# A two-block transformer kernel on one core: one plain fp32 matmul per dense product in place of three matmuls over high and low halves

## The chip, the core and the metric

The kernel runs on one NeuronCore of a Trainium2 chip. Five engines work side by side, each with a program of its own, and meet only at semaphores: TensorE (PE, matmuls and transposes, with weight loads shown apart as PEld), VectorE (DVE), ScalarE (ACT), GpSimd (POOL) and SyncE (SP, which starts the DMAs). The metric is device time in microseconds of one launch. Time before: 4109.65 us, the median of three runs between 4104.24 and 4113.88.

## What is computed

There are 16 sequences of 512 tokens and 256 channels. Each goes through two residual blocks, cut here to what matters:

```python
x = x + attn(layernorm(x))      # 16 heads of 16 channels: q, k, v = x @ Wq.T, x @ Wk.T, x @ Wv.T
                                # layernorm of q and k per head, causal softmax, out @ Wo.T + bo
x = x + ffn(layernorm(x))
# ffn: y = y + latent attention(rmsnorm(y)): q = y @ Wq (16 heads of 64),
#      ckv = y @ Wkva (64 wide), causal softmax, Wkvb, @ Wo
#      y = y + shared expert + sum over the 2 chosen of 8 experts, each silu(y @ Wg) * (y @ Wu) @ Wd
```

All inputs and outputs are fp32. The dense products are the q, k, v and output projections of both attentions, the gate's logits, and the nine experts (one shared, eight routed). The kernel computes all nine for all tokens and weighs them.

## The kernel before

One sequence is one pass of a loop ("batch" b, 16 passes; the last one is written out apart). Tokens lie in NT = 4 tiles of 128, channels in KC = 2 halves of 128. The weights are loaded, scaled and centred once before the loop, and stay in SBUF. Every engine runs its own hand-written order, and semaphores (the `Signal` objects) tie them.

**How a dense product is made.** PE has two ways to take fp32 data. Tiles declared `F32R` go in as one instruction. Tiles declared `F32` go in as a plain fp32 matmul. Here every dense operand is held twice, as a high half (a copy rounded to fp32r) and a low half (what is left over), and a product is the sum of three fp32r matmuls, `TERMS`: high by high, high by low, low by high. The weights' halves are made before the loop (ACT copies at L811, DVE subtractions at L1016). The tokens' halves are made three times per batch, after PE has transposed the normalised tokens into PSUM: ACT copies `xth` (L818), DVE subtracts `xtl` (L1032). The halves of an attention's output are `oth` (ACT, L851) and `otl` (POOL, L462; the last of four by DVE, L1087), from `onm` (L1068). Those of an expert's hidden layer are `hidh` (ACT, L958) and `hidl` (DVE, L1218), from `hid` (L1214).

**A batch on PE, in order.** (1) `project_qk` (L566) and `project_v` (L575) for four token tiles; `transpose_stack` (L590). (2) `attend` for the first attention: scores (L602, L608), transposes of the probabilities (L619), `weigh_values` (L630), sums (L639), then `project_out` (L671). (3) `transpose_tokens` (L551), then eight `project_q` (L691), each with a `transpose_q` (L704) of two steps earlier, and one `project_kv` (L679). (4) `attend` for the second attention with scores at L606 and L607, then `project_out`. (5) `transpose_tokens`, the gate (L777), and the experts: `gate_up(e + 1)` (L717, two products of 256 by 512 tokens) stands ahead of `down(e)` (L729). Next to `down(8)` stands the transposition of the next batch's tokens.

**What the other engines do beside it.** ACT: exponentials (L833), every third to fourth copy of a probability block (L841), SiLU (L954). DVE: row maxima (L1049), the other block copies (L1057), and per expert `hid`, `hidl` and four additions into `x1` (L1230). POOL: the powers of -1/2 (L449), the spread of the sums (L457), rotary sums (L499) and the key's parts (L506 to L516).

`weigh_values` (L630) and the two products that fold weights before the loop (L537, L542) already use plain fp32 tiles (`va`, `vb`, `probt`; `r_wqt`, `r_kvbt`, `r_wob`). In the trace a plain fp32 matmul stands as two MATMUL records with a weight load each, and an fp32r matmul as one: L630 issues 2560 matmuls in each attention over the run, and the trace has 5120 records for each.

## Time and profile before

| what | value |
|---|---|
| median of three runs | 4109.65 us |
| span of the profiled execution | 4099.4 us |
| PE busy | 3512.7 us (86%), 31392 matmul records |
| DVE busy | 3056.1 us (75%) |
| ACT busy | 2303.1 us (56%) |
| POOL busy | 776.0 us (19%) |
| length of one batch (the second, by the returning pattern of instructions) | 249.2 us |
| start of the first matmul of batch 0 | 86.56 us |

The page has one line per engine with its busy time, a chain of work that ended last with each engine's share of it, and groups of instructions by source line. A matmul's duration includes its way through the array, so consecutive matmuls overlap in the records, and the distance between two starts tells what one costs. PEclk is the clock that PE was granted, as a share of 2.4 GHz: 1.00 is 2.4 GHz and 0.50 is 1.2 GHz.

### The profile page before, as it was taken

The page shows a single profiled execution, that of the slowest core. Times are in us where ns is not written, and L with a number is a line of the kernel's source. Part 1 is how long each engine was busy: PE and PEld are TensorE (multiplying, and loading weights), DVE is VectorE, ACT ScalarE, POOL GpSimd, SP SyncE. Part 2 cuts the span into 40 slices and gives each one's busy share as a digit, 9 for nine tenths or more (in the row PEclk, how much of TensorE's full clock was granted, in tenths as well). Part 3 has the DMA queues.
Part 4 walks back from the last instruction along what each step waited for, and adds up shares of the span by engine and source line. Part 5 has one row for each costly group of instructions (what it writes and reads, how often), then busy time and mean ns, then how long its engine had stood idle before and what let it go on. Part 6 is the DMA issues. An engine that isn't in the chain of part 4 may idle for free.

```text
span 4099.4 us, 93010 instructions
## 1 busy us (share of the span) xinstructions
PE 3512.7 (86%) x31392; PEld 2772.0 (68%) x31392; DVE 3056.1 (75%) x6444; ACT 2303.1 (56%) x6346; POOL 776.0 (19%) x919
## 2 busy tenths in 40 slices
PE   3898988989889898898988889888898988989888
PEld 2676766767667676676766767666676766767667
DVE  3878777787777877768787787877778777787776
ACT  2656546565465664646655465654656546565464
POOL 1212222022120221212122121222202212022120
PEclk9999999999899999999999999998999989999899
DMA  3000000000000000000000000000000000000000
GB/s 73 7 2 7 7 7 7 2 7 7 7 7 1 8 6 7 7 7 7 2 7 7 7 7 2 7 7 7 7 2 7 7 7 7 2 7 7 6 1 6
DMA packets 33906, 30.35 MB, mean 7 GB/s; under 512 B 8864, under 2 KB 33312, under 8 KB 33376
## 3 DMA queue, kind: packets, MB, share of 16 engines
q1 hardware_dynamic: 33376, 23.68, 2.0%
q8 instruction: 284, 4.65, 0.5%
q14 instruction: 246, 2.02, 0.2%
HBM read 15.28 MB, written 8.39 MB: 6 GB/s over the span
## 4 chain that ended last, share of the span: by engine, by line
PE 56%; issue 14%; DVE 13%; ACT 10%; POOL 5%; SPq 1%; ACTq 0%; DMA 0%; DVEq 0%; POOLq 0%
PE bank L619 12%; PE scores L717 9%; ACT prob L833 6%; PE bank L630 6%; PE scores L606 6%; PE bank L729 5%; PE scores L607 4%; PE scores L608 3%; POOL qf L499 2%; PE scores L691 2%; PE scores L671 2%; PE scores L602 2%; PE bank L590 2%; DVE negmax L1049 1%; DVE stk L1145 1%
## 5 line engine op out<-in xcount | busy, mean ns | idle before, releaser
L833 ACT ACTIVATE prob<-scores,negmax 128x128 f32<-128x128 f32 (+3 forms) x2048 | 1060.8, 538 | 223.6 <-DVE negmax L1049 180.2
L1049 DVE TENSOR_REDUCE negmax<-scores 128x1 f32<-128x128 f32 (+3 forms) x2048 | 884.5, 483 | 102.0 <-PE scores L608 88.4
L619 PE MATMUL bank<-ident,prob 128*128 128x128 f32 x5120 | 731.2, 280 | 44.5 <-DVE probt L1057 35.1
L1057 DVE COPY probt<-bank 128x512 f32<-128x512 f32 x896 | 596.6, 683 | 180.1 <-PE bank L619 173.1
L619 PEld LDWEIGHTS bank<-ident,prob 128*128 128x128 f32 x5120 | 548.6, 142 | 155.5 <-DVE probt L1057 65.9
L606 PE MATMUL scores<-khh,qt 128*128 128x256 f32 (+2 forms) x1024 | 439.2, 430 | 13.3 <-issue 6.6
L608 PE MATMUL scores<-mask,ident 128*128 128x128 bf16 x2048 | 450.4, 231 | 0.0
L833 ACT ACTIVATION_READ_ACCUMULATOR prob<-scores,negmax 128x1 f32 x2048 | 438.0, 214 | 0.0
L804 ACT ACTIVATE probt<-bank 128x512 f32<-128x512 f32 x384 | 233.0, 607 | 205.3 <-PE bank L619 205.3
L607 PE MATMUL scores<-kll,qt 128*128 128x256 f32 (+2 forms) x1024 | 346.1, 338 | 0.0
L590 PE MATMUL bank<-ident,stk 128*96 128x128 bf16 x2048 | 206.9, 288 | 149.8 <-DVE stk L1147 119.7
L717 PE MATMUL scores<-xth,wgu 128*128 128x512 f32 x1152 | 328.2, 407 | 0.0
L602 PE MATMUL scores<-qkt 96*128 96x128 bf16 (+3 forms) x1024 | 266.5, 306 | 45.9 <-DVE qkt L1037 13.9
L590 PEld LDWEIGHTS bank<-ident,stk 128*96 128x96 bf16 x2048 | 191.4, 178 | 166.0 <-DVE stk L1147 78.1
L608 PEld LDWEIGHTS scores<-mask,ident 128*128 128x128 bf16 x2048 | 205.4, 100 | 141.4 <-issue 110.7
L462 POOL TENSOR_TENSOR otl<-onm,oth 128x512 fp32r<-128x512 f32 x96 | 122.6, 1277 | 897.0 <-ACT oth L804 897.0
L717 PEld LDWEIGHTS scores<-xth,wgu 128*128 128x128 f32 x1152 | 214.0, 194 | 43.8
L954 ACT ACTIVATE sg<-scores 128x512 f32<-128x512 f32 x144 | 86.3, 599 | 279.0 <-PE scores L717 279.0
L457 POOL COPY rexp<-rsum 128x512 f32<-128x512 f32 x128 | 78.3, 612 | 859.7 <-DVE rsum L1061 859.7
L449 POOL TENSOR_TENSOR rstd<-var,expo 128x4 f32<-128x4 f32 x64 | 66.9, 1052 | 898.3 <-DVE var L1109 551.6
L729 PE MATMUL bank<-wd,hidh 128*128 128x256 f32 x1152 | 212.0, 282 | 27.4 <-ACT hidh L804 21.8
L606 PEld LDWEIGHTS scores<-khh,qt 128*128 128x128 f32 x1024 | 221.1, 216 | 17.9 <-issue 9.6
(178 smaller groups left out, 6937.0 us busy)
## 6 DMA issues: line engine op xcount, KB each, us to landing
x_in<-in_x_rows SPq DMA_DIRECT2D x16, 512.0 KB, 3.5
out_rows<-x SPq DMA_DIRECT2D x16, 512.0 KB, 3.5
r_gu<-in_wg SPq DMA_DIRECT2D x2, 512.0 KB, 5.1
r_gu<-in_wu SPq DMA_DIRECT2D x2, 512.0 KB, 5.1
r_d<-in_wd SPq DMA_DIRECT2D x1, 1024.0 KB, 6.5
r_wqt<-in_wq_nope_t SPq DMA_DIRECT2D x1, 512.0 KB, 6.8
r_wqr<-in_wq SPq DMA_DIRECT2D x2, 256.0 KB, 8.6
r_wob<-in_wo SPq DMA_DIRECT2D x1, 512.0 KB, 5.3
```

The lines of the kernel that those rows point to most:

```text
L590: ins = nc.tensor.transpose(out[0:SD, i * P:(i + 1) * P], stk[:, t % 2, quad * 8 + i].rearrange("p s d -> p (s d)"), ident16[:, :])
L602: mm(bank[q][:, 0:n], qkt[:, h, j * P:(j + 1) * P], qkt[:, H + h, 0:n], start=True, stop=False)
L606: mm(bank[q][:, 0:m], tok, khh[:, 0:m], start=True, stop=False)
L607: mm(bank[q][:, 0:m], tok, kll[:, 0:m], start=False, stop=False)
L608: ins = mm(bank[q][:, n - P:n], ident16[:, :], mask16[:, :], start=False, stop=True)
L619: ins = nc.tensor.transpose(bank[4 + n % 2][:, q * P:(q + 1) * P], prob[:, u % 2, q, i * P:(i + 1) * P], ident[:, :])
L630: ins = mm(bank[6][q * HP:(q + 1) * HP, j * P:(j + 1) * P], val, probt[:, u % 2, i, q * P:(q + 1) * P], start=i == 0, stop=i == j)
L717: ins = mm(bank[2 * s + w][:, :], wgu[:, w_, e, k, w * I:(w + 1) * I], XT[x_][:, k], start=m == 0 and k == 0, stop=m == 2 and k == KC - 1)
L729: ins = mm(bank[4 + 2 * s + t // 2][:, (t % 2) * C:(t % 2 + 1) * C], (hidh, hidl)[x_][:, s, t * P:(t + 1) * P], wd[:, w_, e], start=m == 0 ...
L833: nc.scalar.activation(prob[:, u % 2, q, 0:n], bank[q][:, 0:n], ACT.Exp, bias=negmax[:, a, u, q:q + 1], accum_out=sums[:, a, u, q:q + 1]). ...
L1049: nc.vector.tensor_reduce(negmax[:, a, u, M * part:M * part + M], scores[:, M * part:M * part + M, 0:n], axis=AX.X, op=ALU.max, negate=Tru ...
L1057: nc.vector.tensor_copy(probt[:, u % 2, i], bank[4 + n % 2][:, :]).then_inc(probt_dve.sem, 1)
```

## The change

Every dense weight becomes one `F32` tile, and so do the transposed tokens (`xt`), an attention's output (`ot`) and the hidden layer (`hid`). A product is one plain fp32 matmul in place of three fp32r ones. The steps that made halves are gone: the ACT copies and DVE subtractions of the weights, `oth` and `otl`, `hidh` and `hidl`. DVE now writes `ot` where it wrote `onm`. The transposed tokens are copied once, half 0 by ACT and half 1 by DVE, and PE waits for each half where it first needs it. The weights are loaded straight into their final tiles, so the separate raw tiles are gone as well. The attentions' own matmuls (scores, transposes, `weigh_values`) are as before. `weights_ready` is reached after DVE's last scaling (L1011). The core of the diff:

```diff
-    wqkv = new("wqkv", [P, 2, KC, 3 * C], F32R)
...
-    wgu = new("wgu", [P, 2, NE, KC, 2 * I], F32R)
...
+    wqkv = new("wqkv", [P, KC, 3 * C], F32)
...
+    wgu = new("wgu", [P, NE, KC, 2 * I], F32)
...
-    TERMS = ((0, 0), (0, 1), (1, 0))
...
-        sp.wait_ge(weights_ready, len(SPLIT))
+        sp.wait_ge(weights_ready, WEIGHTS)
...
-                if g == NG - 1:
-                    break
-                pool.wait_ge(oth_ready.sem, oth_ready.at(b, a * NG + g + 1))
-                nc.gpsimd.tensor_tensor(otl[:, g], onm[:, :], oth[:, g].bitcast(F32), ALU.subtract).then_inc(otl_ready.sem, 1)
...
-            for m, (x_, w_) in enumerate(TERMS):
-                if t == 0 and m == 2:
-                    lo_split(b, 0)
-                for k in range(KC):
-                    ins = mm(bank[t][:, :], XT[x_][:, k, t * P:(t + 1) * P], wqkv[:, w_, k, 0:2 * C],
-                             start=m == 0 and k == 0, stop=m == 2 and k == KC - 1)
+            for k in range(KC):
+                if t == 0:
+                    tokens_copied(b, 0, k)
+                ins = mm(bank[t][:, :], xt[:, k, t * P:(t + 1) * P], wqkv[:, k, 0:2 * C], start=k == 0, stop=k == KC - 1)
...
             for t in range(NT):
                 for g in groups:
                     if t == 0:
-                        pe.wait_ge(oth_ready.sem, oth_ready.at(b, a * NG + g + 1))
-                        pe.wait_ge(otl_ready.sem, otl_ready.at(b, a * NG + g + 1))
-                    for m, (x_, w_) in enumerate(TERMS):
-                        ins = mm(bank[t][:, 0:C], (oth, otl)[x_][:, g, t * P:(t + 1) * P], w[:, w_, g],
-                                 start=m == 0 and g == 0, stop=m == 2 and g == NG - 1)
+                        pe.wait_ge(ot_ready.sem, ot_ready.at(b, a * NG + g + 1))
+                    ins = mm(bank[t][:, 0:C], ot[:, g, t * P:(t + 1) * P], w[:, g], start=g == 0, stop=g == NG - 1)
                 if g == NG - 1:
                     ins.then_inc(y_psum.sem, 1)
...
             if e >= 2:
                 pe.wait_ge(hid_ready.sem, hid_ready.at(b, e - 1))
             for w in range(2):
-                for m, (x_, w_) in enumerate(TERMS):
-                    for k in range(KC):
-                        ins = mm(bank[2 * s + w][:, :], wgu[:, w_, e, k, w * I:(w + 1) * I], XT[x_][:, k],
-                                 start=m == 0 and k == 0, stop=m == 2 and k == KC - 1)
+                for k in range(KC):
+                    ins = mm(bank[2 * s + w][:, :], wgu[:, e, k, w * I:(w + 1) * I], xt[:, k], start=k == 0, stop=k == KC - 1)
             ins.then_inc(gate_up_psum.sem, 1)
 
         def down(b, e):
             s = e % 2
-            pe.wait_ge(hidh_ready.sem, hidh_ready.at(b, e + 1))
-            pe.wait_ge(hidl_ready.sem, hidl_ready.at(b, e + 1))
+            pe.wait_ge(hid_ready.sem, hid_ready.at(b, e + 1))
             if e >= 2:
                 pe.wait_ge(down_added.sem, down_added.at(b, e - 1))
             for t in range(NT):
-                for m, (x_, w_) in enumerate(TERMS):
-                    ins = mm(bank[4 + 2 * s + t // 2][:, (t % 2) * C:(t % 2 + 1) * C], (hidh, hidl)[x_][:, s, t * P:(t + 1) * P],
-                             wd[:, w_, e], start=m == 0, stop=m == 2)
+                ins = mm(bank[4 + 2 * s + t // 2][:, (t % 2) * C:(t % 2 + 1) * C], hid[:, s, t * P:(t + 1) * P], wd[:, e],
+                         start=True, stop=True)
                 if t % 2:
                     ins.then_inc(down_psum.sem, 1)
...
-        def split_tokens(b, stage):
-            for k in range(KC):
-                act.wait_ge(xt_psum.sem, xt_psum.at(b, stage * KC + k + 1))
-                copy(xth[:, k], bank[TOKEN_BANK[stage] + k][:, :]).then_inc(xth_ready.sem, 1)
+        def copy_tokens(b, stage):
+            act.wait_ge(xt_psum.sem, xt_psum.at(b, stage * KC + 1))
+            copy(xt[:, 0], bank[TOKEN_BANK[stage]][:, :]).then_inc(xt_act.sem, 1)
...
-        def split_out(b, a, g):
-            act.wait_ge(onm_ready.sem, onm_ready.at(b, a * NG + g + 1))
-            copy(oth[:, g], onm[:, :]).then_inc(oth_ready.sem, 1)
...
                 act.wait_ge(gate_up_psum.sem, gate_up_psum.at(b, e + 1))
+                if e >= 2:
+                    act.wait_ge(hid_ready.sem, hid_ready.at(b, e - 1))
                 nc.scalar.activation(sg[:, s], bank[2 * s][:, :], ACT.Silu).then_inc(silu_ready.sem, 1)
-                act.wait_ge(hid_ready.sem, hid_ready.at(b, e + 1))
-                if e >= 2:
-                    act.wait_ge(down_psum.sem, down_psum.at(b, 2 * (e - 1)))
-                copy(hidh[:, s], hid[:, s]).then_inc(hidh_ready.sem, 1)
...
-        for n, (raw, w, _) in enumerate(SPLIT):
-            dve.wait_ge(hi_ready, n + 1)
-            raw_ = raw[tuple([slice(None)] * len(raw.shape))]
-            tt(flat(w[:, 1]), flat(raw_), flat(w[:, 0]).bitcast(F32), ALU.subtract).then_inc(weights_ready, 1)
+            ins = ts(wgate[:, k], wgate[:, k], r_ln[:, 1, k:k + 1], None, ALU.mult)
+        ins.then_inc(weights_ready, 1)
...
-        def split_tokens(b, stage):
-            for k in range(KC):
-                dve.wait_ge(xth_ready.sem, xth_ready.at(b, stage * KC + k + 1))
-                tt(xtl[:, k], bank[TOKEN_BANK[stage] + k][:, :], xth[:, k].bitcast(F32), ALU.subtract).then_inc(xtl_ready.sem, 1)
+        def copy_tokens(b, stage):
+            dve.wait_ge(xt_psum.sem, xt_psum.at(b, (stage + 1) * KC))
+            nc.vector.tensor_copy(xt[:, 1], bank[TOKEN_BANK[stage] + 1][:, :]).then_inc(xt_dve.sem, 1)
...
-            if g > 0:
-                dve.wait_ge(otl_ready.sem, otl_ready.at(b, a * NG + g))
-            tt(onm[:, :], bank[7][:, :], osb[:, :], ALU.mult).then_inc(onm_ready.sem, 1)
+            tt(ot[:, g], bank[7][:, :], osb[:, :], ALU.mult).then_inc(ot_ready.sem, 1)
...
-            dve.wait_ge(oth_ready.sem, oth_ready.at(b, (a + 1) * NG))
-            tt(otl[:, NG - 1], onm[:, :], oth[:, NG - 1].bitcast(F32), ALU.subtract).then_inc(otl_ready.sem, 1)
...
-                    dve.wait_ge(hidh_ready.sem, hidh_ready.at(b, e + 1))
-                    if e >= 2:
-                        dve.wait_ge(down_psum.sem, down_psum.at(b, 2 * (e - 1)))
-                    tt(hidl[:, s], hid[:, s], hidh[:, s].bitcast(F32), ALU.subtract).then_inc(hidl_ready.sem, 1)
```

PE, in the experts: one `down` and the `gate_up` behind it, before (`scores` and `bank` are PSUM).

```order
L729 MATMUL bank<-wd,hidh 128x256 x2
L729 MATMUL bank<-wd,hidl 128x256
L729 MATMUL bank<-wd,hidh 128x256 x2
L729 MATMUL bank<-wd,hidl 128x256
L729 MATMUL bank<-wd,hidh 128x256 x2
L729 MATMUL bank<-wd,hidl 128x256
L729 MATMUL bank<-wd,hidh 128x256 x2
L729 MATMUL bank<-wd,hidl 128x256
L717 MATMUL scores<-xth,wgu 128x512 x4
L717 MATMUL scores<-xtl,wgu 128x512 x2
L717 MATMUL scores<-xth,wgu 128x512 x4
L717 MATMUL scores<-xtl,wgu 128x512 x2
```

The same place of the changed kernel, with the `gate_up` ahead of it and the next `down`:

```order
L632 MATMUL scores<-xt,wgu 128x512 x4
L637 REGISTER_ALU
L641 MATMUL bank<-wd,hid 128x256 x4
L632 MATMUL scores<-xt,wgu 128x512 x4
L637 REGISTER_ALU
L641 MATMUL bank<-wd,hid 128x256 x4
```

Twelve matmuls of 256 columns became four plain ones, and twelve of 512 columns became four; their order is the same.

ACT, at the end of the experts and the hand-over to the next batch, before:

```order
L954 ACTIVATE sg<-scores 128x512
L957 REGISTER_ALU
L804 ACTIVATE hidh<-hid 128x512
L817 ISA
L804 ACTIVATE xth<-scores 128x512
L817 REGISTER_ALU
L804 ACTIVATE xth<-scores 128x512
L961 ACT_TABLE_LOAD
```

And of the changed kernel:

```order
L847 ACTIVATE sg<-scores 128x512
L844 REGISTER_ALU
L847 ACTIVATE sg<-scores 128x512
L715 ISA
L710 ACTIVATE xt<-scores 128x512
L850 ACT_TABLE_LOAD
```

The copy between two SiLUs is gone, and one of the two token copies has moved to DVE.

## Rows read from the trace of the kernel before

**Rows 1.** Page, part 1: engine, busy us, share of the span, instructions.

```profile
PE 3512.7 (86%) x31392; PEld 2772.0 (68%) x31392; DVE 3056.1 (75%) x6444; ACT 2303.1 (56%) x6346; POOL 776.0 (19%) x919
```

**Rows 2.** Page, part 4: the chain that ended last, by engine.

```profile
PE 56%; issue 14%; DVE 13%; ACT 10%; POOL 5%; SPq 1%; ACTq 0%; DMA 0%; DVEq 0%; POOLq 0%
```

**Rows 3.** Table by stage, batch 1: stretch, length, busy us (instructions) of PE, PEld, DVE, ACT, POOL; granted clock.

```profile
333.90:366.20 32.30, 20.79 (x147) 18.30 (x148) 27.24 (x45) 17.50 (x34) 13.88 (x22) 0.75 0.06 19
366.20:423.50 57.30, 51.93 (x656) 37.16 (x654) 48.57 (x103) 45.18 (x148) 6.26 (x7) 0.99 0.01 2
435.60:459.30 23.70, 21.51 (x114) 17.02 (x114) 16.48 (x39) 12.18 (x26) 13.59 (x13) 0.94 0.00 0
468.60:526.80 58.20, 57.86 (x663) 44.14 (x661) 46.02 (x92) 41.30 (x133) 6.29 (x7) 0.99 0.01 2
548.07:577.70 29.63, 29.63 (x169) 25.80 (x170) 21.93 (x51) 8.10 (x14) 1.01 (x1) 1.00 0.00 1
```

**Rows 4.** Experts of batch 1: chain in order of time, then timeline with the wait in brackets.

```profile
556.74 1.41 PE bank L729 x12
558.15 2.80 PE scores L717 x12
...
548.07 0.48 PE L729 MATMUL bank<-wd,hidh 128*128 128x256 f32 x2 [0.56 <-DVE hidl L1218]
```

**Rows 5.** Timeline; single lines (forms, ns min/median/max, first and last start); table by stage.

```profile
276.69 1.08 PE L630 MATMUL bank<-probt,vb 128*32 128x128 f32 x32
...
L630 PE MATMUL bank<-probt,vb x320: 272/273/297, 221.9 to 277.5; 128*32 128x128 f32 x160
...
L729 PE MATMUL bank<-wd,hidh x72: 278/279/360, 548.1 to 582.7; 128*128 128x256 f32 x72
...
L542 PE MATMUL scores<-r_wob,r_kvbt x32: 629/629/630, 51.2 to 54.2; 32*32 32x256 f32 x32
...
L777 PE MATMUL scores<-xtl,wgate x2: 628/628/628, 539.5 to 539.9; 128*8 128x512 f32 x2
...
538.00:540.00 2.00, 2.00 (x6) 0.52 (x4) 1.74 (x3) 0.00 (x0) 0.00 (x0) 0.50 0.00 0
```

**Rows 6.** Timeline of PE before the first batch.

```profile
37.45 13.86 PE L537 MATMUL scores<-r_kvbt,r_wqt 32*128 32x32 f32 x64 [37.45 <-DMA r_woa<-in_wo1t]
```

**Rows 7.** Chain in order of time, before the first batch.

```profile
62.26 1.13 DVE woa L1016
...
76.00 0.10 DVE wgate L1016
```

**Rows 8.** Timeline of DVE beside the second output projection of batch 1.

```profile
529.08 0.69 DVE L1087 TENSOR_TENSOR otl<-onm,oth 128x512 fp32r<-128x512 f32 x1 [0.70 <-ACT oth L804]
```

**Rows 9.** Timeline where tokens go from PE through ACT and DVE back to PE.

```profile
434.48 1.09 ACT L804 ACTIVATE xth<-bank 128x512 fp32r<-128x512 f32 x2 [8.78 <-PE bank L551]
...
435.62 2.07 PE L691 MATMUL scores<-wq,xth 128*128 128x512 f32 x4 [0.96 <-ACT xth L804]
```

**Rows 10.** Timeline of the query projections, batch 1: the starts of two in a row.

```profile
449.65 1.18 PE L691 MATMUL scores<-wq,xth 128*128 128x512 f32 x4
...
451.91 1.18 PE L691 MATMUL scores<-wq,xth 128*128 128x512 f32 x4
```

**Rows 11.** Turn from batch 1 to batch 2: timeline, then chain.

```profile
581.45 0.47 PE L729 MATMUL bank<-wd,hidh 128*128 128x256 f32 x2 [1.36 <-ACT hidh L804]
...
583.10 2.38 issue
585.49 2.94 PE scores L566 x6
```

**Rows 12.** Timeline of ACT in the first attention of batch 1.

```profile
375.78 0.60 ACT L804 ACTIVATE probt<-bank 128x512 f32<-128x512 f32 x1
...
388.80 0.61 ACT L804 ACTIVATE probt<-bank 128x512 f32<-128x512 f32 x1
...
402.06 0.61 ACT L804 ACTIVATE probt<-bank 128x512 f32<-128x512 f32 x1
```

167 lines of the change are left out of this document (58 added, 109 removed).

## The prediction

> **What bounds the kernel now.** I began with the busy times and the chain that ended last. PE is busy for 86% of the span [rows 1], and 56% of the chain is PE's own work; DVE has 13%, ACT 10%, POOL 5% [rows 2]. So PE's work counts, but not everywhere, and the table by stage says where [rows 3]. In the experts PE is busy for all 29.63 us. In the second attention it is busy for 57.86 of 58.20 us, in the first for 51.93 of 57.30 us. In the stretch of the q, k, v projections and their norms (333.9 to 366.2) it is busy for 20.79 of 32.30 us only: there a chain through ACT, DVE and POOL sets the pace. In the query projections it is busy for 21.51 of 23.70 us. Last I read the chain inside the experts [rows 4]: `down` 1.41 us, `gate_up` 2.80 us, in turn and with nothing between.
>
> **What a plain fp32 matmul costs.** This decides the case. An fp32r `gate_up` is 12 matmuls of 512 columns in 2.80 us, 0.233 us each; a `down` is 12 of 256 columns in 1.41 us, 0.1175 us each [rows 4]. Both are 0.457 ns per column: call that one pass. `weigh_values` shows the plain form. Its row has 32 records for 16 matmuls, each of 128 columns over a strip 32 wide [rows 5]. Four strips run side by side, so the 32 starts make 28 steps: (1.08 - 0.27) / 28 = 0.029 us per record, or four times that, 0.116 us, for 128 columns in one strip. That is 0.90 ns per column and record, two passes, so two records are four passes. The durations agree: a plain record of 128 columns takes 273 ns and an fp32r one of 256 columns 279 ns [rows 5]. At the lower clock (granted 0.50, which is 1.2 GHz) an fp32r matmul of 512 columns takes 628 ns, and a plain record of 256 columns before the first batch takes 629 ns [rows 5]. So a product goes from three passes to four: a third of the matmuls stays in the code, and PE's dense work grows by a third.
>
> **The change part by part, for one batch.**
>
> Experts. One pass of a `gate_up` is 2.80 / 3 = 0.933 us, of a `down` 1.41 / 3 = 0.47 us. Nine of each add 12.6 us. From this go two waits of PE. Before `down(0)` it waits 0.56 us for `hidl` [rows 4]; `hid` alone is ready earlier, and PE comes later. Before `down(8)` it waits 1.36 us for `hidh` [rows 11]; without the copy, and with DVE no longer held behind it, `hid(8)` is ready before PE has transposed the next tokens. In between the removed steps save nothing, as PE never waits there. Net 12.6 - 1.9 = +10.7 us. DVE would be next, with 21.93 us for some seven experts [rows 3], about 3.1 us each with `hidl` in it, against 5.6 us of PE.
>
> Output projections. Each is 16 products of 256 columns, 16 x 0.1175 = 1.9 us more, twice: +3.7 us. The halves of the last group are hidden before: PE starts the projection when the attention's stretch ends, at 526.8 [rows 3], and its first two groups of channels are 24 matmuls, 2.8 us, to 529.6; `otl` is written from 529.08 to 529.77 [rows 8]. So their removal gives at most 0.2 us back, which I leave out; PE's own work is late next.
>
> Query projections. Nine products of 1024 columns (eight queries, one key and value) add 9 x 0.47 = 4.2 us. Two starts in a row are 2.26 us apart [rows 10]: 1.40 us of projection and eight transposes at 0.117 us, 0.94 us, with nothing free. But early and late in the stretch PE waits for rotary sums and copies, in all 2.2 us [rows 3]. I let half of it absorb work: +3.1 us. The bounds are +2.0 and +4.2.
>
> q, k, v projections. The extra pass is 6144 columns, 2.8 us. All but the first tile lies under the 11.5 us that PE idles in that stretch [rows 3]. The first tile, now 2.94 us at the lower clock for most of it [rows 11], is waited for. If the clock comes back after as long a time as now, what is added runs at the upper level: +0.4 us. The bounds are 0 and +2.8.
>
> Gate. One product of 1024 columns, waited for and at the lower clock. By the same reasoning +0.3 us; +0.9 us if all of it stays at 1.2 GHz.
>
> Hand-over of tokens. Now ACT copies both halves in 1.09 us and PE starts after the second [rows 9]. Afterwards PE starts after ACT's first, with DVE's copy beside it: -0.45 us before the queries and before the gate. At the turn of the loop PE's own 2.38 us of issue [rows 11] hides this hand-over already, so nothing there.
>
> Attentions. ACT no longer makes `oth`. In the first attention the same copy comes back after 13.02 us where no `oth` lies between and after 13.26 us where one does [rows 12], so three are worth 0.7 us. In the second, PE has no gap to give [rows 3]. POOL's `otl` has slack. -0.7 us, with 0 and -4 (all six copies of 0.65 us) as bounds.
>
> Before the loop. DVE's subtractions run from 62.26 to 76.10 us on the chain [rows 7], and the first token load waits for them. They go, and so do ACT's copies beside them: -13.8 us once.
>
> Sum per batch: 10.7 + 3.7 + 3.1 + 0.4 + 0.3 - 0.9 - 0.7 = +16.6 us. Over 16 batches that is +266 us; less 13.8 it is +252 us. The span goes from 4099.4 to 4351 us. The median of the runs stands 10.25 us above the span, so I say **4361 us**.
>
> **Rivals.**
>
> Faster. A plain record costs one pass, not two, when all 128 columns of the array are used, so that a product is two passes instead of three. `weigh_values` would then be slow for another reason, its 0.029 us between starts being a limit of issue. For it: no row shows a plain matmul 128 rows deep and 128 columns wide. Against it: the 629 ns of L542 beside the 628 ns of an fp32r matmul twice as long. Then a pass is saved where I add one: experts 12.6 and their waits 1.9, outputs 3.7, the rest with hand-overs and attention about 2, some 20 us per batch, and 4109.65 - 320 - 14 = 3775 us. What the change gives apart from passes (before the loop 0.9, waits 1.9, hand-overs 0.9, attention 0.7) is 4.4 us per batch, and one pass is worth about 20 us (12.6 + 3.7 + 3.1 + 0.4 + 0.3). So faster begins where a product costs less than about 3.2 passes.
>
> Much slower by the weight loads. Each plain record loads its own weights. L537 gives the price of a load 128 wide: (13.86 - 0.40) / 63 = 0.214 us per record at the lower clock [rows 6], thus 0.107 us at the upper. If that stood ahead of each record instead of under the one before, 280 records per batch, some 80% of them exposed, would cost 24 us: 16 x 24 = 383, in all about 4740 us. Against it: the fp32r `down` loads weights 128 wide for each matmul and still runs at 0.1175 us [rows 4], which leaves no room for a load of 0.107 us outside.
> The Trainium skill ("TensorE: Matmul & The Clock Gate", Measured speedup vs the span model) says that a weight load overlaps a matmul in flight only where the row group differs. By this rule the rival holds; the fp32r rows already go against it.
>
> Much slower by the clock. The plain matmuls before the first batch fill PE for 17.5 us, and the last still take 629 ns [rows 5, 6], the duration of the lower level. If plain matmuls did not hold 2.4 GHz, experts and output projections would cost twice their four passes: 9 x 4 x 1.40 = 50 us and 15 us per batch, 16 x 65 = 1040 us more, about 5400 us. Against it: those used 32 of 128 rows, while `weigh_values` runs at the upper level among other work.
>
> **How the numbers follow.** The forecast has 85%, the faster rival 5%, the weight loads 5%, the clock 3%; 2% is for what I don't see. The range holds the forecast's own bounds. Low: queries +2.0, attention -1.9, and one lower-clock stretch each gone before the first projection and before the stack (-2.2 together): 12.1 us per batch, 4289 us. High: nothing absorbed (queries +4.2, first projections +2.8, gate +0.9, half of the experts' waits kept, no gain in attention): 22.4 us, 4454 us. I take 4289 to 4454. The rivals lie far outside it and hold 13%. A measurement of this kernel can tell about 0.2% from no change; faster by more than that 5%, within it 1%, slower by more 94%.
>
> **What would show it.** Right: a `gate_up` of 8 records in about 3.74 us and a `down` of 8 in 1.87 us, gapless, at granted clock 1.00; the two halves of an attention nearly unchanged; the first token load near 62 us; a batch of about 265.8 us against 249.2. Wrong: a plain record of 512 columns well under 0.45 us after its neighbour, idle time or longer steps between a load and its matmul, or a granted clock of 0.50 inside the experts.

## The result: 60 us slower, a quarter of what was forecast

The changed kernel takes 4170.77 us, the median of four runs between 4168.76 and 4173.19. The kernel before, on the same chip, takes 4111.36 us (four runs, 4104.24 to 4113.88). The ratio is 1.0157, with a 95% interval from 1.0125 to 1.0188 (the two medians alone give 1.0145). I had said 4361 us, within 4289 to 4454. The sign is right and the size is four times too large, outside the range by 118 us. The span of the profiled execution is 4168.9 us, 69.5 us above the 4099.4 us of before.

The page of the changed kernel, part 1 (busy us, share of the span, instructions) and part 4 (the chain that ended last, by engine), answers to [rows 1] and [rows 2]:

```profile
PE 3685.4 (88%) x29152; PEld 2557.2 (61%) x29152; DVE 2880.1 (69%) x6212; ACT 2112.5 (51%) x6017; POOL 647.3 (16%) x823
...
PE 60%; DVE 15%; issue 14%; POOL 5%; ACT 4%; SPq 1%; DVEq 0%; DMA 0%; POOLq 0%; ACTq 0%
```

PE is busy for 173 us more; DVE is busy for 176 us less and ACT for 191. ACT's share of the chain fell from 10% to 4%, PE's rose from 56% to 60%. The other engines gave time back, but PE was the one that was waited for.

The chain inside the experts, against [rows 4]:

```profile
556.72 1.73 PE bank L641 x8
558.45 3.43 PE scores L632 x8
```

The products stand without a gap, as forecast, but a `gate_up` takes 3.43 us where I had 3.74, and a `down` 1.73 where I had 1.87. This is the largest error. An eighth of 3.43 us is 0.429 us for a record of 512 columns.

Timelines of two query projections in a row [rows 10], of the first output projection, and of the gate [rows 5, 9]:

```profile
444.53 1.88 PE L607 MATMUL scores<-wq,xt 128*128 128x512 f32 x4
446.25 1.04 PE L620 MATMUL bank<-ident,stq 128*128 128x128 f32 x8
447.12 1.88 PE L607 MATMUL scores<-wq,xt 128*128 128x512 f32 x4
...
413.59 7.17 PE L590 MATMUL scores<-woa,ot 128*128 128x256 f32 x32
...
531.15 1.88 PE L684 MATMUL scores<-xt,wgate 128*8 128x512 f32 x4 [0.58 <-ACT xt L710]
```

A query projection with its eight transposes takes 447.12 - 444.53 = 2.59 us from start to start, against 2.26 before [rows 10]. The gate now waits 0.58 us for the token copy where it waited 1.07, and its four records take 1.88 us together. That is the pace of the upper clock level. The same place of the kernel before, timeline:

```profile
537.83 1.88 PE L777 MATMUL scores<-xth,wgate 128*8 128x512 f32 x4 [1.07 <-ACT xth L804]
```

There the 1.88 us are four fp32r matmuls, half as fast as in a `gate_up`, where twelve take 2.80 us.

The clock shows in a table by stretch (length, busy us of PE, PEld, DVE, ACT, POOL; then the granted clock, the DMA share and GB/s). First the gate in the kernel before, then the gate, the first two `gate_up` and the turn of the loop in the changed one:

```profile
537.80:541.60 3.80, 3.00 (x10) 0.92 (x10) 1.94 (x3) 0.59 (x1) 0.00 (x0) 0.57 0.00 0
```

```profile
531.10:534.10 3.00, 2.19 (x8) 0.60 (x8) 1.33 (x2) 0.59 (x1) 0.00 (x0) 1.00 0.00 0
534.10:541.10 7.00, 7.00 (x19) 3.17 (x18) 4.04 (x13) 2.11 (x3) 0.00 (x0) 1.00 0.01 2
577.00:588.00 11.00, 10.02 (x40) 6.53 (x39) 5.61 (x13) 4.22 (x8) 2.76 (x6) 1.00 0.16 54
```

The gate ran at 0.57 of 2.4 GHz before, that is nearly all at 1.2 GHz, and runs at 2.4 GHz in this execution. Over the whole run the trace has 622 us at the lower level before and 413 us after.

The turn from batch 1 to batch 2, a timeline with waits in brackets, answers to [rows 11]:

```profile
578.92 1.04 PE L478 MATMUL scores<-ident,xn 128*128 128x128 f32 x8
579.80 1.89 PE L641 MATMUL bank<-wd,hid 128*128 128x256 f32 x8
582.67 3.69 PE L490 MATMUL scores<-wqkv,xt 128*128 128x512 f32 x8 [0.98 <-issue]
```

The wait of 1.36 us before `down(8)` is gone, as forecast. The 2.38 us of issue behind it became 0.98 us, which I had not forecast. The records of PE's sequencer, the part that waits, branches and issues, show what this is. Here is its record of the loop's branch back to the start of the next pass, at this turn, by source line (ns, then the start in us), for the kernel before and the changed one:

```profile
L794 PEldq COMPARE_BRANCH  x1: 3665/3665/3665, 581.7 to 581.7; - x1
```

```profile
L701 PEldq COMPARE_BRANCH  x1: 3618/3618/3618, 578.9 to 578.9; - x1
```

The branch takes as long in both. Before, the sequencer stood at the wait and came to the branch 0.2 us after `down(8)` had started; now it comes there 0.9 us ahead of it, and more of the branch lies under PE's work. The next projection starts 0.17 us after the branch ends in both (585.49 and 582.67).

Before the loop, the chain in order of time, against [rows 7]:

```profile
60.98 0.28 DVE wgate L891 x2
...
61.28 3.29 DMA x_in<-in_x_rows
...
70.90 3.80 PE scores L490 x4
```

The first token load starts at 61.28 us (I had said near 62), and the first projection at 70.90 us instead of 86.56.

For the whole run I divided each batch at the first start of each PE group and took the mean over the 15 looped batches, in us; the last row but one gives the first start of all, the last one the time at the lower level in the whole run. The kernels of the later columns are the experiments below; a name is the label without its suffix.

| stage | before | after | e1 | e2 | e3 | e4 | e5 | e8 | e9b |
|---|---|---|---|---|---|---|---|---|---|
| q, k, v to first stack transpose | 14.58 | 14.34 | 14.54 | 15.00 | 15.11 | 14.69 | 14.60 | 14.65 | 14.42 |
| stack transposes | 18.71 | 18.77 | 18.25 | 18.84 | 18.22 | 18.46 | 18.18 | 18.32 | 18.55 |
| first attention | 54.39 | 53.64 | 54.28 | 54.48 | 53.64 | 53.81 | 53.66 | 54.24 | 53.73 |
| output projection, norm | 9.33 | 10.63 | 11.16 | 9.42 | 10.63 | 10.63 | 10.63 | 9.27 | 10.64 |
| token hand-over | 2.88 | 2.35 | 2.84 | 2.84 | 2.03 | 2.69 | 2.07 | 2.47 | 1.99 |
| queries | 28.20 | 29.93 | 31.35 | 28.68 | 30.15 | 30.10 | 30.02 | 26.65 | 27.63 |
| second attention | 63.55 | 63.01 | 62.64 | 63.10 | 61.94 | 61.11 | 62.26 | 62.87 | 62.89 |
| output projection, norm | 8.62 | 9.92 | 10.52 | 8.71 | 9.93 | 9.92 | 9.92 | 8.67 | 9.93 |
| token hand-over | 2.40 | 1.85 | 2.29 | 2.07 | 2.81 | 2.91 | 2.10 | 2.29 | 1.80 |
| gate | 3.89 | 2.99 | 4.52 | 3.97 | 3.89 | 4.62 | 3.76 | 2.64 | 2.96 |
| `gate_up` 0 and 1 | 7.13 | 6.97 | 7.57 | 6.97 | 7.15 | 6.97 | 6.97 | 6.42 | 6.97 |
| `down(0)` to the last transposes | 30.98 | 37.84 | 41.23 | 37.85 | 30.97 | 37.85 | 37.85 | 30.98 | 37.85 |
| turn (transposes, `down(8)`, branch) | 6.20 | 3.66 | 5.07 | 3.65 | 6.10 | 3.62 | 5.51 | 6.20 | 3.58 |
| a batch | 250.86 | 255.91 | 266.25 | 255.59 | 252.57 | 257.39 | 257.53 | 245.68 | 252.93 |
| first projection of batch 0 starts | 86.56 | 70.90 | 87.20 | 77.83 | 80.77 | 71.21 | 70.75 | 86.63 | 70.70 |
| time at 1.2 GHz in the run | 622 | 413 | 408 | 587 | 465 | 467 | 376 | 366 | 281 |

The lower clock level falls on other stages in other executions of one kernel, so a single stage of this table is uncertain by up to 0.9 us where PE runs at either level (gate, hand-overs, queries, second attention). The sum of a batch is not: a second profile of the changed kernel, below, gives 255.86 us against 255.91.

### The profile page after: what moved, and what is told of

The parts are those of the page before. It is cut to its first block, busy times and chain, and to the rows that moved or that the text cites. A ratio compares the mean times of both kernels' runs of the same rounds, so it can differ in the third digit from the quotient of the medians.

```text
span 4168.9 us, 87466 instructions
## 1 busy us (share of the span) xinstructions
PE 3685.4 (88%) x29152; PEld 2557.2 (61%) x29152; DVE 2880.1 (69%) x6212; ACT 2112.5 (51%) x6017; POOL 647.3 (16%) x823
## 4 chain that ended last, share of the span: by engine, by line
PE 60%; DVE 15%; issue 14%; POOL 5%; ACT 4%; SPq 1%; DVEq 0%; DMA 0%; POOLq 0%; ACTq 0%
PE scores L632 12%; PE bank L540 11%; PE bank L641 6%; PE scores L527 5%; PE bank L551 5%; DVE negmax L924 5%; PE scores L528 4%; PE scores L590 3%; PE scores L529 3%; POOL qf L429 2%; PE bank L511 2%; PE scores L607 2%; DVE probt L932 2%; DVE stk L1015 1%; PE scores L523 1%
## 5 line engine op out<-in xcount | busy, mean ns | idle before, releaser
L632 PE MATMUL scores<-xt,wgu 128*128 128x512 f32 x1152 | 516.9, 594 | 0.0
L731 ACT ACTIVATION_READ_ACCUMULATOR prob<-scores,negmax 128x1 f32 x2048 | 424.3, 207 | 0.0
L632 PEld LDWEIGHTS scores<-xt,wgu 128*128 128x128 f32 x1152 | 217.9, 190 | 220.1 <-issue 214.1
L511 PE MATMUL bank<-ident,stk 128*96 128x128 bf16 x2048 | 197.8, 282 | 145.4 <-DVE stk L1017 117.1
L1083 DVE TENSOR_TENSOR hid<-scores,sg 128x512 f32<-128x512 f32 x144 | 99.6, 691 | 327.3 <-ACT sg L847 327.3
L607 PE MATMUL scores<-wq,xt 128*128 128x512 f32 x512 | 266.1, 652 | 8.0 <-ACT xt L710 8.0
L641 PE MATMUL bank<-wd,hid 128*128 128x256 f32 x1152 | 272.0, 379 | 0.0
L641 PEld LDWEIGHTS bank<-wd,hid 128*128 128x128 f32 x1152 | 218.0, 190 | 83.3 <-issue 61.1
```

The costliest lines, as they stand in the source:

```text
L511: ins = nc.tensor.transpose(out[0:SD, i * P:(i + 1) * P], stk[:, t % 2, quad * 8 + i].rearrange("p s d -> p (s d)"), ident16[:, :])
L607: ins = mm(bank[n % 4][:, :], xt[:, k, t * P:(t + 1) * P], wq2[:, k, w * 8:(w + 1) * 8].rearrange("p h d -> p (h d)"), start=k == 0, stop= ...
L632: ins = mm(bank[2 * s + w][:, :], wgu[:, e, k, w * I:(w + 1) * I], xt[:, k], start=k == 0, stop=k == KC - 1)
L641: ins = mm(bank[4 + 2 * s + t // 2][:, (t % 2) * C:(t % 2 + 1) * C], hid[:, s, t * P:(t + 1) * P], wd[:, e], start=True, stop=True)
L731: nc.scalar.activation(prob[:, u % 2, q, 0:n], bank[q][:, 0:n], ACT.Exp, bias=negmax[:, a, u, q:q + 1], accum_out=sums[:, a, u, q:q + 1]). ...
```

## The experiments

Three questions were open. What does a plain fp32 matmul cost, and how did I misread it? Where do the 2.5 us at the turn come from? And what part of the result is the clock's?

### A real fourth pass (e1_fourth_pass)

The forecast came down to a fourth fp32r pass. This kernel is the kernel before with that pass, low by low, in every dense product; nothing else is changed.

```diff
-    TERMS = ((0, 0), (0, 1), (1, 0))
+    TERMS = ((0, 0), (0, 1), (1, 0), (1, 1))
...
-                             start=m == 0 and k == 0, stop=m == 2 and k == KC - 1)
+                             start=m == 0 and k == 0, stop=m == 3 and k == KC - 1)
```

> The kernel before with a fourth fp32r matmul in every dense product (low by low), so that each product is four passes as in the changed kernel, but in the fp32r form, with all halves still made. The record priced the plain form exactly so. Theory A (the plain form streams a pass faster than fp32r does, 0.418 against 0.457 ns per column): a gate_up takes 3.73 us and a down 1.88 us here, against 3.43 and 1.73 us in the changed kernel, and the time is about 4111 + 16 x 19 = 4415 us. Rival B (four passes cost what they cost in the changed kernel whatever the form, and the record's error lies in waits and clock alone): gate_up 3.43 us, time near 4200 us. On the clock: if more PE work alone keeps PE at 2.4 GHz, the time at the lower level falls from 622 us to about 410 us here too; if it is the shorter hand-overs of the changed kernel, it stays near 620 us.

Measured: 4349.35 us, ratio 1.0616 (1.0588 to 1.0644). The chain inside the experts:

```profile
577.57 3.73 PE scores L717 x16
581.30 1.88 PE bank L729 x16
```

These are the 3.74 and 1.87 us of my forecast. So what failed is the identity of a plain fp32 matmul with four fp32r passes: it costs 3.43 / 3.73 = 0.92 of that. The rival that four passes cost 3.43 us in either form falls.

That the whole run lies 12 us from my 4361 us is luck. This kernel still makes all halves, so none of the savings that my sum takes off apply, and by my own price of a pass (some 20 us per batch) it should take 4109.65 + 16 x 20.1 = 4431 us; the text above says 4415. A batch grew by 15.4 us. In the table the output projections (+3.7) and the queries (+3.2) grew as priced, and so did the inner experts (+10.2); but the first two `gate_up` grew by 0.4 us instead of 1.9, the turn shrank by 1.1 and the second attention by 0.9.

The run also answers on the clock: with the hand-overs as long as before (2.84 and 2.29 us), the time at 1.2 GHz fell from 622 to 408 us. More work of PE's own brings that total down with every step kept (it also shortens the wait before `down(8)`, to 0.17 us). The gate stayed at the lower level (4.52 us).

### The parts of the change alone (e2, e3, e7)

In these kernels each dense product is made in the old or in the new way, group by group. The core of the edit:

```diff
+PLAIN = ("exp",)
...
+    def terms(group):
+        return ((0, 0),) if group in PLAIN else TERMS
...
+        def tok(group, x_, k):
+            return xt[:, k] if group in PLAIN else XT[x_][:, k]
```

In `e2_experts_plain` only the gate and the experts are plain; in `e3_rest_plain` the q, k, v, the output and the query projections; in `e7_qkv_plain` only the q, k, v projections. The steps that make halves go with each group.

> The kernel before with only the gate and the experts in the plain form (their halves not made). Theory A with the table by stage of the two kernels: experts +6.9 us per batch, turn -2.5, gate and hand-over -1.4, that is +3.0 x 16 = 48 us; 7.6 us of subtractions before the loop go, so about 4111 + 40 = 4151 us. The record's price would give +10.0 us per batch and 4263 us. If the parts add up, this run and the one with the projections alone stand together 60 us above the kernel before.

> The kernel before with only the projections of both attentions in the plain form. From the table by stage: output projections +2.6 us per batch, queries +1.7, attentions -1.2, hand-over -0.5, q, k, v and stack -0.2, that is +2.4 x 16 = 38 us; 6.8 us before the loop go, so about 4111 + 31 = 4142 us. The record's terms for these parts sum to +6.1 us per batch, 4202 us.

> The kernel before with only the q, k, v projections in the plain form, the one place where PE idles a third of the stretch. The extra pass should be hidden, and 1.8 us before the loop go: within 0.2% of the kernel before. The record's term for it is +0.4 us per batch, +6 us.

Measured: e2 4169.34 us, ratio 1.0181 (1.0154 to 1.0208); e3 4123.61 us, 1.0062 (1.0041 to 1.0082); e7 4118.38 us, 1.0032 (1.0020 to 1.0044). The chain of e2 in the experts is that of the whole change:

```profile
564.52 3.43 PE scores L755 x8
567.95 1.73 PE bank L771 x8
```

Of the change's cost, the experts carry most: from `down(0)` to the last transposes a batch grows by 6.87 us, and at the turn it shrinks by 2.55 us. The other projections cost less, since in e3 nearly half of what they add comes back in the attentions, and 5.8 us once before the loop. e2 came out 18 us above what was expected and e3 18 us below. The q, k, v projections alone are not free: 12 us (0.32%, where I had expected less than 0.2%). Their first stage takes 0.65 us more in e7, 15.23 us, and the queries behind it 0.69 us more, 28.89.

The parts do not add. 73 us (e2) and 27 us (e3) are 100 us, and the whole is 60 to 66 us. 1.4 us per batch, 22 us in the run, is in the sum of a batch: 4.73 and 1.71 us against 5.05. No stage accounts for it alone. The rest is mostly the kernel before, whose median was 4096.6 us where e2 and e3 were measured and 4104.6 to 4111.4 us beside the whole change.

### The form by itself (e6_forms)

Ahead of batch 0, PE runs rows of identical matmuls in the form before and in the new one, over weights 128 and 32 wide, whose results nothing reads:

```diff
+        for _ in range(32):
+            mm(bank[3][:, 0:512], w32[:, 0:P].bitcast(F32), m32[:, 0:512].bitcast(F32), start=True, stop=True)
+        for _ in range(32):
+            mm(bank[3][:, 0:512], w32[:, 0:P], m32[:, 0:512], start=True, stop=True)
...
+        for _ in range(32):
+            mm(bank[3][:, 0:128], w32[:, 0:P].bitcast(F32), m32[:, 0:128].bitcast(F32), start=True, stop=True)
+        for _ in range(48):
+            mm(bank[3][:, 0:512], w16[:, :], m16[:, 0:512], start=True, stop=True)
```

> The kernel before with rows of identical matmuls put ahead of the first batch, one form after another, results not used: fp32r, plain fp32 and bf16, 512, 256 and 128 columns, weights 128 and 32 wide. It tells what sets the pace of a pass. Theory C (streaming one fp32r column costs about 0.457 ns, and the plain form, which needs two passes per element read, hides that): fp32r 0.234 us at 512 columns with weights of either width, plain 0.428 us per record with either. Rival D (the load of new weights for every matmul slows fp32r): with weights 32 wide fp32r falls towards 0.215 us. If bf16 also runs at 0.234 us, it is not the bytes read per column.

Measured: 4229.65 us (one execution), of which the rows of matmuls are some 125. Timeline of PE. L797, L803, L807 and L811 are plain (two records for a matmul), L799, L801, L805 and L809 are fp32r, L813 is bf16:

```profile
87.33 27.63 PE L797 MATMUL scores<-wqkv,wgu 128*128 128x512 f32 x64
114.40 7.83 PE L799 MATMUL scores<-wqkv,wgu 128*128 128x512 f32 x32
122.06 7.58 PE L801 MATMUL scores<-wqkv,wgu 128*32 128x512 f32 x32
129.57 27.66 PE L803 MATMUL scores<-wqkv,wgu 128*32 128x512 f32 x64
157.16 7.94 PE L805 MATMUL scores<-wqkv,wgu 128*128 128x256 f32 x64
164.93 13.98 PE L807 MATMUL scores<-wqkv,wgu 128*128 128x256 f32 x64
178.56 7.45 PE L809 MATMUL scores<-wqkv,wgu 128*128 128x128 f32 x64
185.84 7.36 PE L811 MATMUL scores<-wqkv,wgu 128*128 128x128 f32 x64
193.26 10.74 PE L813 MATMUL scores<-wqkv,ident 128*128 128x512 bf16 x47
```

The granted clock is 1.00 in all of them. A row's length less one record, over the number of steps, gives the cost of a record: (27.63 - 0.59) / 63 = 0.429 us for L797. (The distance from one row's start to the next misleads, since a record behind one of another form can start early: the first of L799 starts 28 ns after the last of L797, and its second 632 ns later.) The middle step between two starts within a row, in ns:

| columns | fp32r, 128 wide | fp32r, 32 wide | plain, 128 wide | plain, 32 wide | bf16, 128 wide |
|---|---|---|---|---|---|
| 512 | 227 | 231 | 429 | 429 | 225 |
| 256 | 120 | | 216 | | |
| 128 | 111 | | 112 | | |

This shows the mistake. At 512 and 256 columns a plain record costs 0.84 ns per column, 1.89 and 1.80 times an fp32r record, not twice (in the kernel, where an fp32r record of 512 columns takes 233 ns, it is 1.84 times). At 128 columns it costs 112 ns, 0.88 ns per column, and an fp32r record of 128 columns costs as much. Below 256 columns something else sets the pace, the same in both forms. My price of 0.90 ns per column came from `weigh_values` [rows 5], which has records of 128 columns: I had measured that floor. The width of the weights is not the cause at 512 columns: with weights 32 wide both forms keep their pace, so the rival that the weight load slows fp32r falls.

From 256 to 512 columns an fp32r record adds 107 ns and a plain one 213, exactly twice. The forms differ by a part that does not grow with the columns: 13 ns in an fp32r record (120 - 107) and 3 ns in a plain one (216 - 213), worked out from these rows. At the lower clock level it does not show. In the query projections that ran at 1.2 GHz the middle step is 427 ns for an fp32r record of 512 columns (kernel before, 59 steps) and 854 ns for a plain one (changed kernel, 48 steps): there the forecast's four passes are right. Why the part is there at the upper level is not settled, nor what the floor of some 112 ns is. A hint lies in [rows 6]: records of only 32 columns over weights 128 wide take 214 ns at the lower level, 107 if halved, close to that floor.

### Where the turn's gain comes from (e5_halves_kept)

The changed kernel, but ACT and DVE make `hidh` and `hidl` as before and PE waits for both. Its products still read `hid`; the two tiles are only waited for, and the output is computed as in the changed kernel.

```diff
-            pe.wait_ge(hid_ready.sem, hid_ready.at(b, e + 1))
+            pe.wait_ge(hidh_ready.sem, hidh_ready.at(b, e + 1))
+            pe.wait_ge(hidl_ready.sem, hidl_ready.at(b, e + 1))
...
+                copy(hidh[:, s], hid[:, s]).then_inc(hidh_ready.sem, 1)
...
+                    tt(hidl[:, s], hid[:, s], hidh[:, s], ALU.subtract).then_inc(hidl_ready.sem, 1)
```

> The changed kernel with the expert's hidden layer still copied by ACT and subtracted by DVE as before, PE waiting for both, while the matmul still takes the whole value in plain form. It tells what taking these steps away is worth at four passes. If the turn's 2.5 us (6.20 to 3.66 us from the last transposes' start to the next batch) come from them, the turn goes back to 5 to 6 us and the time rises by 16 x 2 = 32 us to about 4200 us. If PE's own longer work would hide them anyway, the time stays within 5 us of the changed kernel's 4171 us.

Measured: 4194.52 us, ratio 1.0217 (1.0192 to 1.0241); the changed kernel has 1.0157 and 1.0171 in its two comparisons. The medians lie 24 us apart, and the sum of a batch grew by 1.62 us, 26 us in the run. The turn in e5, against the rows above:

```profile
578.51 1.04 PE L482 MATMUL scores<-ident,xn 128*128 128x128 f32 x8
580.22 1.96 PE L646 MATMUL bank<-wd,hid 128*128 128x256 f32 x8 [0.67 <-issue]
584.05 3.70 PE L494 MATMUL scores<-wqkv,xt 128*128 128x512 f32 x8 [1.87 <-issue]
```

From the transposes to the next projection it is 5.54 us, against 3.75 without these steps. With the wait comes 0.9 us of issue behind `down(8)`. The loop's branch in e5, and at the same turn in e1:

```profile
L706 PEldq COMPARE_BRANCH  x1: 3561/3561/3561, 580.3 to 580.3; - x1
```

```profile
L794 PEldq COMPARE_BRANCH  x1: 3925/3925/3925, 618.1 to 618.1; - x1
```

So the 2.38 us of issue in [rows 11] were the end of the loop's branch, and how much of it shows depends on when the sequencer comes to it. With the wait back it starts 0.1 us after `down(8)` instead of 0.9 us before. In e1 `down(8)` starts at 617.95 after an idle time of only 0.17 us, the branch follows it by 0.2 us, and the issue is 2.14 us. So the wait need not be long: in e1 the sequencer stood at its semaphore for 2.2 us all the same. In the kernel before, in e5 and in e1 it was held until `down(8)` could start, and nearly the whole branch came behind that. The inner experts, 37.85 us, do not change, so the halves were hidden there, as forecast.

### The tokens' hand-over (e4_act_copies_both)

The changed kernel, but ACT copies both halves of the tokens and PE waits for both.

```diff
-            copied = xt_dve if k else xt_act
-            pe.wait_ge(copied.sem, copied.at(b, stage + 1))
+            pe.wait_ge(xt_act.sem, xt_act.at(b, 2 * stage + 2))
...
+            act.wait_ge(xt_psum.sem, xt_psum.at(b, (stage + 1) * KC))
+            copy(xt[:, 1], bank[TOKEN_BANK[stage] + 1][:, :]).then_inc(xt_act.sem, 1)
```

> The changed kernel with both halves of the transposed tokens copied by ACT, as before the change, and PE waiting for both. Theory A: +0.45 us at each of two hand-overs, 16 x 0.9 = 14 us, 4185 us. If it is the shorter gap before the gate that keeps PE's clock up there (granted 1.00 in most batches of the changed kernel, 0.50 in the kernel before), the gate falls back to the lower level and costs 1 us more per batch: about 4201 us, and the time at the lower level rises from 413 to about 470 us.

Measured: 4193.70 us, ratio 1.0236 (1.0210 to 1.0263); the median is 23 us above the changed kernel's. That lies between the 14 us of the copies alone and the 30 us with the gate at the lower level. The hand-overs of the two stages grow by 0.34 and 1.06 us, and the gate by 1.63 us, against the first profile of the changed kernel. Its timeline:

```profile
534.90 3.50 PE L683 MATMUL scores<-xt,wgate 128*8 128x512 f32 x4 [0.96 <-ACT xt L709]
```

The wait is 0.96 us instead of 0.58, and the four records take 3.50 us instead of 1.88: the same matmuls, at the lower clock level. In e4 the gate takes over 4.5 us in all 16 batches. In the changed kernel it takes over 4.2 us in one of 16 in the first profile, and in nine of 16 in a second one (e11b below). So the longer pause goes with the lower level at the gate, but the first profile alone makes it look too clear. In the table the second attention gives 1.9 us back in this run, so the stages alone don't make the sum; the sum of a batch grows by 1.5 us. The turn is unchanged (3.62 against 3.66 us), so the hand-over is hidden there, as forecast.

### Holding the clock (e8_fill_gaps, e9b_after_filled)

If the lower level is a cost of its own, it can be bought off in the kernel before as well. In e8 the kernel before runs small bf16 matmuls, which nothing reads, while PE waits for the norm and for the tokens' copies:

```diff
+        def fill(n):
+            for _ in range(n):
+                mm(bank[7][:, 0:P], ident16[:, :], mask16[:, :], start=True, stop=True)
...
+            fill(52)
             transpose_tokens(b, 1)
+            fill(12)
             hi_split(b, 1)
...
+            fill(40)
             transpose_tokens(b, 2)
+            fill(12)
             hi_split(b, 2)
```

> The kernel before, unchanged but for bf16 matmuls of 128 columns whose results nobody reads, put where PE waits for the norms after each output projection (52 and 12 after the first, 40 and 12 after the second). It tests the clock by itself. If PE's waits are what lets its clock fall to 1.2 GHz before the queries and the gate, the transposes, the first query product and the gate run at 2.4 GHz: gate 3.9 to 2.9 us, hand-overs 2.9 to 2.2 and 2.4 to 2.2 us, first query 1.2 us less, the time at the lower level down by 200 us or more, and the whole about 16 x 3 = 48 us (1.2%) faster than before. If the clock falls for another reason, the time is the same or a little longer.

Measured: 4020.20 us, ratio 0.9788 (0.9766 to 0.9810), 86 us less where 48 were expected. It beats both kernels. Timeline at the second hand-over:

```profile
527.57 2.41 PE L664 MATMUL bank<-mask,ident 128*128 128x128 bf16 x40
530.47 1.23 PE L551 MATMUL bank<-ident,xn 128*128 128x128 f32 x8 [0.50 <-DVE xn L1196]
531.54 0.83 PE L664 MATMUL bank<-mask,ident 128*128 128x128 bf16 x12
532.76 1.10 PE L785 MATMUL scores<-xth,wgate 128*8 128x512 f32 x4 [0.39 <-ACT xth L812]
```

The table of that stretch:

```profile
527.57:535.40 7.83, 6.17 (x72) 4.54 (x70) 4.16 (x9) 2.63 (x7) 1.02 (x1) 1.00 0.00 0
```

PE idles 0.50 us before the transposes instead of 2.75, as the fills take up the rest, the granted clock is 1.00 where it had been 0.57 at the gate, and the first four records of the gate take 1.10 us where they took 1.88. Nothing else of the kernel is touched. Per batch the queries give 1.55 us, the gate 1.25, the first two `gate_up` 0.71, the second attention 0.68, the hand-overs 0.52: 4.7 of the 5.2 us.

In e9b the changed kernel gets the same fills (52 and 4 at the queries, 40 and 4 at the gate, as its second wait is shorter):

```diff
+            fill(52)
             transpose_tokens(b, 1)
+            fill(4)
...
+            fill(40)
             transpose_tokens(b, 2)
+            fill(4)
```

> The changed kernel with the same unread bf16 matmuls at the same places as in the filled kernel before (52 and 4, 40 and 4). The filled kernel before gained 5.2 us per batch. If the changed kernel had that gain already in part, through its shorter hand-overs and longer matmuls, it gains less here, 16 x 2 = 32 us to about 4140 us; and with the clock held in both kernels the change costs about 4140 - 4020 = 120 us, twice what it costs without. If the clock had no part in the small loss measured, both gain alike and this one comes to about 4087 us.

Measured: 4128.71 us, ratio 1.0069 (1.0045 to 1.0093). Spans and mean granted clocks of the profiled executions of before, after, e8 and e9b, in this order:

```profile
core 0: 4099.4 us, clock 0.924
```

```profile
core 0: 4168.9 us, clock 0.951
```

```profile
core 0: 4018.2 us, clock 0.955
```

```profile
core 0: 4117.2 us, clock 0.966
```

The kernel before gains 86 us from the fills, the changed one 42. With the pauses filled in both, the change costs 4128.7 - 4020.2 = 108 us; without, 60 to 66. So some 45 us of the difference are the clock's: the changed kernel is granted 2.4 GHz for more of the run. The clock is not held alike in the two filled kernels (366 and 281 us remain at the lower level), so this is a rough figure, not a bound.

### Fills before the stack as well (e10b_fill_stack)

e8 with 64 and 40 more fills ahead of the first and third `transpose_stack`, where PE waits for DVE:

```diff
+            pe.wait_ge(qn_ready.sem, qn_ready.at(b, 1))
             for t in range(NT):
+                fill((64, 0, 40, 0)[t], k=0)
                 transpose_stack(b, t)
```

> The filled kernel before with 64 and 40 more such matmuls ahead of the first and the third stack transposition, where PE waits for the norms of q and k and the granted clock is 0.50 for some 10 us per batch. If the transposes there are on the path and slow for the clock, 8 transposes take 0.47 us in place of 0.87 us, worth 1 to 2 us per batch: about 4000 us. If the chain through ACT, DVE and POOL covers them, the time stays at 4020 us, or rises by what the fillers delay.

Measured: 4033.74 us, ratio 0.9826 (0.9797 to 0.9854); 14 us above e8, where 20 us less were hoped for. The time at 1.2 GHz fell from 366 to 246 us and the mean clock rose from 0.955 to 0.970, but nothing was gained. Divided as in the table, a batch is only 0.07 us shorter than in e8 up to the start of the first attention: PE is not the one that is waited for there, so a faster PE buys next to nothing. The loss is at the turn, which grew from 6.20 to 7.30 us. The loop's branch in e8 and e10b over the run (shortest, middle and longest in ns):

```profile
L802 PEldq COMPARE_BRANCH  x15: 83/3522/3932, 329.3 to 3770.6; - x15
```

```profile
L804 PEldq COMPARE_BRANCH  x15: 83/4757/5108, 328.7 to 3786.1; - x15
```

The branch takes 1.2 us longer. Why it does is not shown. (The 83 ns are the last turn, where the loop is left.) The granted clock is no aim by itself.

### The changed kernel again (e11b_after_again)

The changed kernel as it is, on the chip of e9b and e10b.

> The changed kernel once more, so that it shares the runs of the kernel before with the filled kernels: about 1.6% slower than before again.

Measured: 4170.55 us, ratio 1.0171 (1.0141 to 1.0200). In this profile the gate takes 3.84 us instead of 2.99, with the same sum of a batch (255.86 us) and nearly the same time at 1.2 GHz (410 us). So the gain at the gate that the first profile shows is not to be taken by itself: the lower level had fallen elsewhere. What stays from one execution to the next is its total.

## Why the prediction was wrong, point by point

Per batch, in us; "at the measured price" is my own sum with 3.43 and 1.73 us in place of 3.74 and 1.87.

| step | forecast | at the measured price | measured |
|---|---|---|---|
| experts and turn | +10.7 | +6.6 | +4.2 |
| output projections | +3.7 | +2.6 | +2.6 |
| queries | +3.1 | +1.8 | +1.7 |
| q, k, v and stack | +0.4 | +0.4 | -0.2 |
| gate | +0.3 | +0.3 | -0.9 |
| hand-overs | -0.9 | -0.9 | -1.1 |
| attentions | -0.7 | -0.7 | -1.3 |
| a batch | +16.6 | +10.1 | +5.0 |
| 16 batches, less what goes before the loop | +252 | +148 | +65 |

**The price of a plain matmul: the step that failed.** I wrote "0.90 ns per column and record, two passes, so two records are four passes". The number was right for `weigh_values` and wrong for records of 256 and 512 columns (0.84 ns). A pass more was to cost 0.933 us in a `gate_up`; it costs 3.43 - 2.80 = 0.63. In a `down` it was 0.47 and is 0.32. So a product costs 3.43 / 2.80 = 1.23 of the old one, not 1.33. This accounts for 104 of the 187 us by which +252 missed +65. The supporting rows deceived me too. The 629 ns for a plain record of 256 columns beside 628 ns for fp32r of 512 were both taken at the lower clock level, where the two forms do stand exactly one to two; the dense products run at the upper level, where they don't. And the 273 ns beside 279 ns came from 128 columns. In the changed kernel a plain record of 512 columns lasts 592 ns and the next starts after 429, where an fp32r record takes 233.

The Trainium skill ("TensorE: Matmul & The Clock Gate", Back-to-back issue gap) gives N / 2.4 + 2.5 ns from one matmul to the next at the upper clock level. For two passes of 512 columns this is an estimate of 432 ns, and the plain rows agree (429). For fp32r it gives 216 ns, and the trace says 233 in this kernel and 227 in e6. Had I held the fp32r rows against it, I would have asked whether the 17 ns above it belong to the plain form too.

**The turn: right in its wait, short in its size.** The wait of 1.36 us went. I had left the issue at 2.38 us, as if it were a fixed piece behind `down(8)`, and it shrank to 0.98, because the loop's branch starts 1.1 us earlier against `down(8)`, which itself lasts 0.3 us longer. e5 brings both back in part. The turn gives 2.54 us per batch; from my own terms, with a `down(8)` longer by 0.32, it would have given 1.04. That is 1.5 us, 24 us in the run.

**The clock: the term that wasn't there.** I let the time at 1.2 GHz stay where it was and only asked at which level added columns would run. It fell by 209 us. e1 has it fall by 214 us with the longer products alone, so PE's own added work is enough for the total; the gate, which stayed at the lower level in e1, needed the shorter hand-over as well, and even then it ran there in nine of 16 batches of the second profile. The steps named by it are the gate (1.2 us per batch below my figure), the first two `gate_up` (7.13 to 6.97 us, where the price of a pass adds 1.26 and the wait for `hidl` takes 0.56, so 0.86 us more than that went), and parts of the first projections and the second attention. e8 and e9b put its share at some 45 us of the run; e11b shows that the single stages can't be trusted for it.

**Where I was right.** The change is slower. A plain product goes from three column times to nearly four, with the weight loads under the matmuls: there is no gap in the experts, so the rival of exposed loads falls, and so do the rival of a single pass and that of a lower clock under plain matmuls (granted 1.00 in the experts' first stretch). The loop starts 15.7 us earlier (13.8 forecast). The first attention gives 0.75 us (0.7 forecast), the hand-overs 0.5 us each (0.45). The halves inside the experts were hidden, and the output projections' last halves too. The queries' gaps absorbed 1.2 us where I assumed 1.1: 9 x 0.32 = 2.9 us added, 1.7 measured. (My reading of that stretch was loose: 1.40 and 0.94 us are more than the 2.26 us from start to start, as a transpose costs 0.109 us there.) The rule of the Trainium skill that I cited for the weight loads stands in "TensorE: Matmul & The Clock Gate" under The mechanism; the fp32r rows went against it, and the plain ones do too.

**A small slip.** I added 10.25 us from the span of the profiled execution to the median. A run stands only 1.9 us above its own span (4170.71 against 4168.9); the profiled execution before was faster than the timed ones. That is 8 us of the 190.

**What stays open.** Why an fp32r record of 512 columns costs more than half a plain one at the upper clock level (12 ns in e6, 18 in the kernel); what sets the floor of some 112 ns at 128 columns; the longer branch in e10b; the 1.4 us per batch by which the two parts exceed the whole.

## What to carry to other kernels

Take the price of a matmul form from a row with the same number of columns, and from the distance of two starts at a known clock: at 128 columns two forms cost the same here that differ by a factor of 1.9 at 512. Take the steps inside one row, not from one row to the next, and take them at the clock level of the work in question. A wait of PE's can cost twice, once itself and once by the clock granted behind it, so count the time at the lower level before and after. And cheap unread matmuls in PE's waits gained 2.1% here, more than any part of the change moved; where PE isn't the one waited for, they gained nothing. At a loop's turn, look at when the sequencer reaches the branch, not only at what PE waits for.

## What the runs showed of the hardware that I had not expected

- At granted clock 1.00 a plain fp32 record costs 429 ns for 512 columns and 216 ns for 256; an fp32r record 227 and 120 ns; a bf16 one (10.74 - 0.39) / 46 = 0.225 us for 512. Per pass the plain form is the faster one. At 1.2 GHz there is no difference: 854 and 427 ns for 512 columns.
- Down at 128 columns both fp32 forms cost about 112 ns per record, while the bf16 fills of 128 columns in e8 take (2.41 - 0.23) / 39 = 0.056 us each, with a duration of 0.23 us for one. Whether the floor is the fp32 weight load was not tried.
- The branch at the end of a pass of the loop holds PE's sequencer for some 3.5 us (3.3 to 3.9 us in the kernel before) while matmuls already started run on; it costs what sticks out behind them, 2.38 us before and 0.98 us after.
- With one more ACT copy ahead of the gate its four matmuls took some 3.5 us in every batch; without it they took 1.88 us in 14 of 16 batches of one execution and in 7 of 16 of another.
- Filling 2 to 3 us pauses of PE twice per batch lowered the time at 1.2 GHz from 622 to 366 us and the run by 2.1%.
